# A macaron block on one NeuronCore: a new order ahead of both expert loops and at the change to the attention, with half-chunk signals and tanh gates

## The reference

```python
x = x + 0.5 * ffn(layernorm(x))       # x is (4, 256, 256): 1024 tokens of 256
x = x + attention(layernorm(x))
x = x + 0.5 * ffn(layernorm(x))

def ffn(x):                            # 8 experts, two for each token
    g, u = split(x @ shared_gate_up_w.T)
    shared = silu(g) * u @ shared_down_w.T             # 704 inner columns
    shared = sigmoid(x @ shared_gate_w.T) * shared
    probs = softmax(x @ gate_w.T); top_w, top_i = top_k(probs, 2)
    top_w = top_w / sum(top_w)
    ye = (silu(x @ w1g[e]) * (x @ w1u[e])) @ w2[e]     # 176 inner columns
    return sum over the two experts of top_w * ye + shared

def attention(x):                      # 16 heads of 128, causal
    q, k, v = x @ W_Q + b_Q, x @ W_K + b_K, x @ W_V + b_V
    return softmax(mask(q @ k.T / sqrt(128))) @ v @ W_O + b_O
```

## Time and profile before

| | us |
|---|---|
| median of three runs | 542.2 |
| lowest and highest | 541.19, 546.09 |
| the profiled execution, its own time | 542.72 |
| its span, first to last instruction | 540.8 |
| PE busy | 515.3 |
| DVE, POOL, ACT busy | 326.7, 273.6, 268.6 |
| f0 (from the trace: PE's first product to the attention's first) | 12.0 to 132.3 |
| attention | 132.3 to 429.1 |
| f1 | 429.1 to 540.8 |

### The profile page before, as it was taken

One profiled execution on the slowest core, in us unless ns is written; L12 is line 12 of the kernel. 1 busy time (PEld: TensorE's weight loads), 2 busy tenths in 40 slices (PEclk: granted clock), 3 DMA queues, 4 the chain that ended last, 5 costly groups with the idle time before them and its releaser, 6 DMA issues. The chain is left out here.

```text
span 540.8 us, 10506 instructions
## 1 busy us (share of the span) xinstructions
PE 515.3 (95%) x3318; PEld 460.3 (85%) x3319; DVE 326.7 (60%) x821; ACT 268.6 (50%) x731; POOL 273.6 (51%) x364
## 2 busy tenths in 40 slices
PE   7999699997989999999999999999999799899996
PEld 4788599976879999898999998999999688799985
DVE  5689655548646564574655645746656768755537
ACT  3982356540554463563544635535456365355540
POOL 1737777751295372570843725718333221667750
PEclk9999799998999999999999999999999999999999
DMA  8941223342101001001010010010000140223327
GB/s 280 348 143 31 68 93 104 107 157 63 55 19 59 1 19 61 19 0 58 19 58 2 18 58 19 0 58 19 0 1 0 49 137 1 69 87 101 106 88 234
DMA packets 19401, 37.99 MB, mean 70 GB/s; under 512 B 2864, under 2 KB 10416, under 8 KB 19376
## 3 DMA queue, kind: packets, MB, share of 16 engines
q1 hardware_dynamic: 14960, 25.61, 14.4%
q0 software_dynamic: 4416, 12.06, 6.9%
HBM read 28.49 MB, written 9.18 MB: 70 GB/s over the span
## 5 line engine op out<-in xcount | busy, mean ns | idle before, releaser
L1315 POOL TENSOR_TENSOR s_a<-s_a,rr_a 128x128 f32<-128x128 f32 x64 | 25.5, 399 | 137.1 <-DVE rr_a L1422 137.1
L1362 ACT ACTIVATE s_a<-s_a,mn_a 128x128 f32<-128x128 f32 (+1 forms) x128 | 56.7, 446 | 14.9 <-DVE mn_a L1416 14.9
L179 PE MATMUL bank<-xT_h,area_h 128*128 128x512 f32 x128 | 53.7, 420 | 3.4 <-PEq L1171 3.4
L1412 DVE SCALAR_TENSOR_TENSOR s_a<-bank,cst 128x384 f32<-128x384 f32 x64 | 35.3, 551 | 35.3 <-PE bank L1533 35.1
L521 POOL DMA_INDIRECT xn<-x_normed,tok_i_f x46 | 45.7, 993 | 16.8 <-issue 10.2
L180 PE MATMUL bank<-xT_l,area_h 128*128 128x512 f32 x128 | 50.8, 397 | 0.0
L181 PE MATMUL bank<-xT_h,area_l 128*128 128x512 f32 x128 | 50.6, 396 | 0.0
L1355 ACT ACTIVATE qk_a<-bank,bias_a 128x512 f32<-128x512 f32 x32 | 21.9, 683 | 55.6 <-PE bank L181 55.6
L1367 ACT ACTIVATE pT_a<-bank 128x384 f32<-128x384 f32 x64 | 31.1, 486 | 34.5 <-PE bank L1542 33.6
L1404 DVE TENSOR_SCALAR qk_a<-bank,bias_a 128x512 f32<-128x512 f32 x32 | 24.0, 751 | 37.5 <-PE bank L181 37.5
L179 PE MATMUL bank<-area_h,xT_h 128*128 128x256 f32 x128 | 40.7, 318 | 0.0
(11 more groups left out here) (176 smaller groups left out, 1652.3 us busy)
## 6 DMA issues: line engine op xcount, KB each, us to landing
area<-in_wqkv SPq DMA_DIRECT2D x8, 768.0 KB, 4.4
xn<-y_by_token SPq DMA_DIRECT2D x12, 256.0 KB, 3.7
w_r<-in_w SPq DMA_DIRECT2D x8, 352.0 KB
area_r<-in_w SPq DMA_DIRECT2D x16, 176.0 KB
x_normed<-xn SPq DMA_DIRECT2D x4, 512.0 KB, 5.8
area<-in_wo SPq DMA_DIRECT2D x8, 256.0 KB, 2.6
x_res<-in_x_in SPq DMA_DIRECT2D x4, 256.0 KB, 4.1
wgu_r<-in_wgu SPq DMA_DIRECT2D x4, 256.0 KB
```

Of the source, the lines that this page charges most:

```text
L179: pe.matmul(psum, lhs[0], rhs[0], start=first, stop=False)
L1362: act.activation(s[b][:, cols], s[b][:, cols], ACT.Exp, bias=mn[:, b, t:t + 1], scale=-1.0, accum_out=rs[:, b, t:t + 1]).then_inc(s_e, 1)
L1412: dve.scalar_tensor_tensor(s[b][:, :], bank[3 + u % 2][:, 0:3 * P], -INV_SCALE, cst[:, C_MASK:C_MASK + 3 * P], ALU.mult, ALU.max).then_inc ...
```

## The change

It touches the order of the work on all five engines and these parts:

- `shared_up(c, g)` is called for each half chunk, and each half signals s_up; so silu(c) waits for g=0 alone. `shared_mul(c)` then waits for the g=1 signal itself.
- In the PE order `route_turn` stands after both halves of chunk 3; chunk 6 (g=0) comes ahead of `ranks`, its g=1 behind; `shared_down` is cut in two parts, and chunk 7's halves stand between; of chunk 8 the second half, and all of chunk 9, follow the first `tile_in`. `up(1)` writes bank 5, so that chunk 9's banks may be in use meanwhile, and one more tile is taken out of the loops.
- POOL does jobs 4, 8, 9, 10, 12 ahead of the token numbers, gathers 0 to 3 as soon as these are there, and then jobs 13, 15, 16, 19, 21, 22. DVE does 11 jobs of f0 where it did 8, and ACT's copies stand in other places.
- The gates are computed by Tanh (0.5 + 0.5 tanh(x/2) is the sigmoid); two DVE operations follow where there were four. A Silu on an unused tile stands at the head of a block, an Exp on it at the end of f0.
- The logits, and A0 of the attention's first round, start with the products of the high part of x, and wait for the low parts only ahead of the last two.
- In f0's tail both `shared_out` of pair 0 stand behind the second pair's statistics, the splitting of the first half for the attention moves behind the meeting of the engines, and the adds of the last four token tiles (8 instructions), the last two `shared_out` and the second half's statistics move into the attention's first round on DVE, around A1 and A3. `shared_down` of the last tiles uses banks 2 and 3 and no longer waits for `shared_out`.
- The attention's masks (196 KB of the constants) are loaded later.

```diff
-POOL_FIRST = {"normed": (2, 3, 5, 6, 7), "assigned": (9, 10, 11), "hot": (12, 13), "gather1": (18,),
-              "gather2": (19,), "gather3": (20, 21, 22)}
-POOL_SECOND = {"normed": (0, 1, 2), "assigned": (3,), "hot": (4, 5)}
+POOL_FIRST = {"start": (1,), "rstd": (4, 8, 9), "assigned": (10, 12), "gather3": (13, 15, 16, 19, 21, 22)}
+POOL_SECOND = {"rstd": (0, 1, 2), "assigned": (3, 4), "gather1": (5,)}
...
 def shared_silu(c):
-    act.wait_ge(s_up, c + 1)
+    act.wait_ge(s_up, ups(c, 0))
...
-def gate_exps():
+def gate_tanhs():
     act.wait_ge(s_route, R1)
-    act.activation(gates[:, 0, :], best2[:, :], ACT.Exp).then_inc(s_exp, 1)
-    act.activation(gates[:, 1, :], lg[:, :, NE], ACT.Exp, scale=-1.0).then_inc(s_exp, 1)
+    act.activation(gates[:, 0, :], best2[:, :], ACT.Tanh, scale=0.5).then_inc(s_exp, 1)
+    act.activation(gates[:, 1, :], lg[:, :, NE], ACT.Tanh, scale=0.5).then_inc(s_exp, 1)
...
 def shared_mul(c):
     dve.wait_ge(s_silu, c + 1)
+    if c % SC < SC - 1:
+        dve.wait_ge(s_up, ups(c, 1))
...
-def shared_up(c, between=None):
+def shared_up(c, g):
     half, ch = divmod(c, SC)
...
+    if c >= 2 and g == 0 and (c - 2) % SC < SC - 1:
+        pe.wait_ge(s_silu, c - 1)
+    elif c >= 2:
+
+        pe.wait_ge(s_hl, c - 1)
...
-                    shared_up(3, route_turn)
-                    shared_up(4)
+                    shared_up(3, 0)
+                    shared_up(3, 1)
+                    route_turn()
+                    shared_up(4, 0)
+                    shared_up(4, 1)
+                    shared_up(5, 0)
+                    shared_up(6, 0)
                     ranks()
-                    shared_up(5)
-                    shared_up(6)
-                    if first:
-                        wait_low(pe, early - 1)
-                    shared_down(0, 0)
-                    shared_up(7)
+                    shared_up(6, 1)
+                    shared_down(0, 0, most)
+                    shared_up(7, 0)
+                    shared_down(0, 0, rest)
+                    shared_up(7, 1)
                     slot_tokens()
-                    shared_down(0, 1)
-                    shared_up(8)
-                    shared_up(9)
+                    shared_up(8, 0)
+                    shared_down(0, 1, most)
+                    shared_down(0, 1, rest)
...
                     tile_in(0, 0)
+                    shared_up(8, 1)
+                    shared_up(9, 0)
+                    shared_up(9, 1)
                     pe.wait_ge(s_hl, SC + AHEAD - 1)
                     tile_in(1, 1)
...
 # attention, DVE
-                    norm_stats(dve, n, 1)
+                    norm_low(dve, n, 0, (4, 5))
                     dve.wait_ge(s_b, 16)
                     dve.tensor_copy(bias[:, :, :], bias_all[:, :, 0:2]).then_inc(s_bp, 1)
+                    dve.wait_ge(s_cst2, 32)
+                    later["adds"](0)
...
+                            if fresh and item == "A3":
+                                later["adds"](1)
+                                later["outs"]()
+                                norm_stats(dve, n, 1)
```

More of the change, by code:

```diff
@@ L38 @@
 AHEAD = 4
-WARM = (24, 4, 8)
+WARM = (20, 3, 8)
 STEPS = 6
@@ L230, in norm_turn, with norm_high @@
                         ins.then_inc(s["xt"], 1)
-        def norm_high(act, s, half, banks):
-            for k in range(KD):
+        def norm_high(act, s, half, banks, ks=range(KD)):
+            for k in ks:
                 act.wait_ge(s["xt"], KD * half + k + 1)
@@ L236, in norm_high, with norm_low @@
                                ACT.Copy).then_inc(s["xth"], 1)
-        def norm_low(dve, s, half, banks):
+        def norm_low(dve, s, half, banks, ks=range(KD)):
             cols = slice(half * HALF, (half + 1) * HALF)
-            for k in range(KD):
+            for k in ks:
                 dve.wait_ge(s["xth"], KD * half + k + 1)
@@ L411, in shared_product, with ups @@
                     return bank[2 * (c % 2)][0:LASTW, :]
+                def ups(c, g):
+                    return sum(2 if a % SC < SC - 1 else 1 for a in range(c)) + g + 1
                 def y_buf(j):
@@ L642, in tile_out @@
                         act.activation(ye[m % YR][:, :], bank[6 + b][:, 0:D], ACT.Copy).then_inc(s_ye, 1)
-                    for m in range(NM + 2):
-                        if 1 < m + 1 < NM:
+                    if first:
+                        act.wait_ge(s_gate_in, 16)
+                        act.activation(flat(wg_h[:, :, :]), wg_raw, ACT.Copy).then_inc(s_gh, 1)
+                        highs("wgh")
+                        norm_high(act, n, 0, (0, 1), (0,))
+                        norm_high(act, n, 0, (0, 1), (1,))
+                        highs("xh1")
@@ L646, in _ @@
+                    inner_high(0, 0)
+                    inner_silu(1, 1, 5)
+                    inner_silu(2, 0)
+                    inner_high(1, 1)
+                    shared_high(9)
+                    tile_high(3, 1)
+                    for m in range(2, NM + 2):
+                        if 3 < m + 1 < NM:
                             tile_high(m + 1, (m + 1) % 2)
-                        if m < NM:
+                        if 2 < m < NM:
                             inner_silu(m, m % 2)
-                        if 0 < m <= NM:
+                        if 2 < m <= NM:
@@ L660, in _ @@
                     if after:
-                        norm_high(act, after, 0, (4, 5))
+                        act.activation(unused[:, :], power[:, 0, :], ACT.Exp)
                 @block.vector
@@ L991, in shared_up, with shared_down @@
+                        for k in range(KD):
+                            at = ch * CH + (g * KD + k) * P
+                            last = split_matmuls(pe, bank[2 * (c % 2) + g][:, :],
+                                                 (wgu_h[:, at:at + P], wgu_l[:, at:at + P]),
+                                                 (xT_h[:, k, toks], xT_l[:, k, toks]), k == 0, k == KD - 1)
                         last.then_inc(s_up, 1)
-                    def shared_down(half, pair):
+                    def shared_down(half, pair, cs):
@@ L994, in shared_down @@
                         j0 = 4 * half + 2 * pair
[L995 to L1012 removed]
+                        if first and not half and not pair and cs[0] == 0:
+                            wait_low(pe, early - 1)
@@ new lines, in shared_down @@
+                        for j in (j0, j0 + 1):
+                            if pair and not half and cs[0] == 0:
+                                pe.wait_ge(s_dnv, j - 1)
+                            toks = slice((j % 4) * P, (j % 4 + 1) * P)
+                            for c in cs:
+                                if j == 4 * half:
+                                    pe.wait_ge(s_hh, SC * half + c + 1)
+                                    pe.wait_ge(s_hl, SC * half + c + 1)
+                                w = P if c < SC - 1 else LASTW
+                                last = split_matmuls(pe, out_bank(j)[:, 0:D],
+                                                     (hT_h[0:w, c, toks], hT_l[0:w, c, toks]),
+                                                     (wd_h[0:w, c, :], wd_l[0:w, c, :]),
+                                                     c == 0, c == SC - 1)
+                            if c == SC - 1:
+                                last.then_inc(s_dn, 1)
@@ L1014, in route_turn @@
+                    most, rest = range(SC - 1), range(SC - 1, SC)
                     def route_turn():
@@ L1162, in _ @@
                     for c in range(SC + AHEAD, 2 * SC):
-                        shared_up(c)
+                        for g in range(2 if c < 2 * SC - 1 else 1):
+                            shared_up(c, g)
                     pe.wait_ge(s_ye, NM)
                     for pair in range(2):
-                        shared_down(1, pair)
+                        shared_down(1, pair, most)
+                        shared_down(1, pair, rest)
                     if after:
```

367 lines of the change are left out of this document (194 added, 173 removed).

## The result

Changed 560.62 us (median of 4), before 543.52 beside it: ratio 1.0324, 95% interval 1.0274 to 1.0375. I had forecast 537.8 in a range of 535.0 to 541.0. The profiled execution of the changed kernel has a span (first to last instruction) of 557.3 us against 540.8. Four marks, each read from a timeline of both traces, split the 16.5 us. `K0` is DVE's first mask of scores in the attention; the trace shows it within 0.3 us of B0 in both kernels.

The account below looks back on a forecast made before the run. PE was taken as busy 515.3 of 540.8 us, with POOL's queue ending f0. Gains of 2.4 (f0), 2.0 (stage) and 0 (f1), 4.4 in all, took 542.7 to 538.3, by median 537.8; range 535.0 to 541.0.

Parts of the forecast that it names:

- f0 up to the token numbers: First expert loop until tok_i is written: tok_i ready at 43.2, 2.65 us earlier.
- the wait at `shared_up(6, 1)`: New PE wait for `shared_low(4)` in both loops: 1.05 us in f0, 1.5 in f1.
- The 0.5 for DVE's early low parts: Total cost allowed for three early DVE low parts meeting POOL's jobs 4 and 8: 0.5 us.
- f0 from there on: First loop behind tok_i: POOL's queue sets the end, last scatter 2.4 us earlier, at 110.6.
- PE's first `up` will come near 53.5: f0: PE's first `up` near 53.5 for 60.26, at full clock, so scatter 0 comes 2.3 us earlier.
- a rule against it: DVE with two SBUF inputs and GpSimd lock a shared port pair: each meeting costs 0 to 2.5 us.
- That POOL's count ends f0: End of f0: POOL's gathers and scatters, 45.27 us from scatter 0 to the last, set it, not PE.
- The change of stage: From f0's first add to B0: 21.8 us for 23.77, so 2.0 us earlier.
- the clock did fall at A0: Rival: PE's clock falls again at A0 or B0, giving 539.0 to 540.5 us; chance 0.22.
- only waits count ... sum 0: f1, first part bound by PE with the same matmuls: waits -1.5 + 0.4 + 1.46 - 0.4, sum 0.
- the rival that they stay: Rival: table loads of 2 x 1.28 us stay between silu(4) and silu(5), giving 543.0 us; chance 0.02.
- The rival on that side: Rival: DVE falls behind, port waits of 2.5 us at jobs 3, 5 and 6: 545.3, with two 542.8; chance 0.06.

Follow-up runs that it names:

- e1: Changed kernel with job 20's high part earlier on ACT and its low part on DVE ahead of POOL's run of low parts: 552.75 us, ratio 1.0157.
- e2: Changed kernel with ACT's high parts of jobs 21 and 22 moved up behind job 20's, job 20 left in place: 561.54 us, ratio 1.0323.
- e5: e1 with the high and low parts of chunk 9 made early, on ACT and DVE, in both expert loops: 550.04 us, ratio 1.0102.
- e12: First loop new and mended, stage and second loop in old order, low parts of jobs 21 and 22 on DVE, not POOL: 539.16 us, ratio 0.9929.
- e13: e1 with ACT's two high parts of the norm's first half ahead of the block's end barrier, on a slower chip: 581.68 us, ratio 1.0131.
- e4: Changed kernel with its change of stage to the attention undone, two `shared_out` of f1's tail going back too: 558.25 us, ratio 1.0243.
- e6: e1 with `shared_up(8, 0)` back behind `shared_down(0, 1)` on PE, in both loops: 563.14 us, ratio 1.0343.
- e10: Kernel before the change with only the gates computed by Tanh instead of Exp: 543.74 us, ratio 1.0014.
- e15: e12 with one more low part, job 19's, made by DVE instead of POOL, on a slower chip: 569.86 us, ratio 0.9924.

## Why the prediction was wrong

- **f0 up to the token numbers: nearly right, in part by luck.** tok_i was ready at 43.8 (43.2 forecast; its own terms, 1.2 and 1.3 off 45.85, make 43.4), after 0.18 us and without table loads at the gates; the wait at `shared_up(6, 1)` was 1.12 (1.05). The logits won 1.72, beyond the bound of 1.3, and the way from there to `ranks` 0.3 where 1.15 was priced, so two misses offset each other. The 0.5 for DVE's early low parts was about right: one took 1.04 us for 0.67 beside a single low part of POOL's.
- **f0 from there on: wrong, 8.2 us.** The failed step is "PE's first `up` will come near 53.5": it came at 61.85, at the lower clock. Of these 8.3 us the hold is 5.9, as e1 shows (55.97); the other 2.5, pauses of PE for gather 0 and for DVE among them, I had left out. I had counted POOL's six low parts in one piece as 8 us on POOL, and not as a time in which DVE can't make one. The mechanism was in my hands, as "a rule against it", but mis-sized: "0 to 2.5" per meeting, and only for jobs 3, 5 and 6 ahead of tok_i. Job 20's meeting cost 5.9 (6.54 less the 0.67 of its twin in the earlier trace rows), because the price goes by the length of POOL's run. The Trainium skill ("SBUF — State Buffer", section "SBUF: two separate sides") has the lock held for one whole instruction; by that an operation waits for one low part, 1.7 us at most here, and 6.54 and 9.00 say otherwise. So did, where I found that the trace agreed: 2.5 us is two of POOL's low parts of 1.24. The second gap of the same step: I took gather 4 as six low parts after gather 3 (57.8), without asking when ACT makes the high parts of 21 and 22; they hung on PE.
- **That POOL's count ends f0: right as a bound, and met only when mended.** In the change PE and POOL are late together: POOL's queue runs without a pause from gather 4 to the last scatter, but gather 4 7.6 us earlier gave nothing (e2), since POOL then waits for PE. With DVE in time, e5 and e12 show POOL's queue as the end.
- **The change of stage: wrong, 4.5 us to `K0` and 5.0 to B0 (26.81 for 21.8).** I had counted 0.35 from the last transposes to the high parts; it is 2.2, for the barrier, which in the kernel before lies behind them and was to be read in the earlier trace rows as `<-PEq`. And the second half's adds, `shared_out` and statistics wait for A1's product (1.82 idle at 141.22), behind an A0 that runs at half clock. Together 3.7 of the 5.0; 0.6 more are the first adds and statistics (5.7 for 5.1, with waits for the read-back), the rest small. That the barrier's share reaches `K0` no run shows (e13 won nothing). The old order of this stage is better by 1.8 in e4, and in every trace. Of the rivals, the clock did fall at A0 (0.77 us for a wide matmul), as in the kernel before.
- **f1: wrong, 8.4 us.** The step "only waits count ... sum 0" priced `shared_up(6, 1)` right (1.48) and the first `up` (its 1.46 went). It left out three: `shared_up(8, 0)` no longer covers high(6) and low(6) behind `shared_down(0, 1)` (1.10, and half clock); the parts of chunk 9, put behind `inner_high(1)`, are late for tile 4 in both loops (2.61, shown by e5 as 3.3 us of f1); and these two stalls bring a stretch at half clock each, 1.6 us, which I had priced at the stage only. e6 adds that the first can't be undone in both loops alone.
- **Tanh: right at nothing.** The loads it removes were covered (e10), and the rival that they stay is out: none stands between Silu and Tanh in either trace.
- **Slower at 0.03** was too low by far. The rival on that side had the right mechanism and looked for it only ahead of tok_i; behind tok_i I walked each engine with the others on time.

## What to carry to other kernels

When work of one engine is gathered into one uninterrupted run, list what the other engine on the same SBUF port does meanwhile: a subtraction with two SBUF inputs ended here only when the run had ended, and everything queued behind it waited. Place it so that it has ended before the run starts (e1), or take work out of the run (e12). For each instruction put later in a queue ask who makes its input and behind what; and look twice at what is put behind a block's barrier though the first work of the next block needs it: A0 waited for it here, though to move the high parts alone back won nothing (e13).

## What the runs showed of the hardware

- DVE's low part (two SBUF inputs) beside a run of POOL's: 6.54 us (run of 5.4), 9.00 (7.8), 3.14 (joined late), each ended 0.56 us after the run. The first two had started 0.62 us ahead of it, beside a gather's issue. Operations of DVE with a PSUM input were not held: in e1 `shared_mul(8)` took 0.70 and `shared_low` twice 1.28 between 52.2 and 54.5, inside POOL's run.
- It isn't only two inputs. In the kernel before, the integer operation of the earlier trace rows has one SBUF input; it took 1.51 us for 0.18 and ended 0.04 us behind the run of the earlier trace rows (45.81), and another (line 775, at 51.65) took 1.80 for 0.17. But a reduction with one (line 723, at 34.91) took 0.22 inside a run of POOL's from 30.55 to 35.58.
- It goes the other way for an issue: gather 0, beside two low parts of DVE's, took 1.75 us for 0.95, and gather 1, beside two more, 1.42.
- A stall of 2.61 us left PE's windows of 4 us behind it at 0.64 (the change, f1) and 0.66 (e1, f0), one of 1.10 at 0.73. One of 1.48 (460.33) left it at 1.00, so the length alone doesn't tell.
- One chip of those used takes 573.9 us for the kernel before instead of 543 to 546. Scatter 0 comes at 67.08 there for 67.09 (e13, e1); the loops are 13 to 16 us longer each (e13 for e1, e15 for e12), with PE idle for up to 2.6 us every few tiles. The ratios came out alike (1.0131 and 1.0157, 0.9924 and 0.9929).
